# A decoder layer on one Trainium2 core: where the first two head groups are loaded, which stores a block waits for, and the order of the first instructions

## The reference

```python
# 1. mixing
pos_mem_cos = cumsum(cos(pp) * (x @ Wpv + bpv)); pos_mem_sin = cumsum(sin(pp) * (x @ Wpv + bpv))
pos_ret = (cos(pp) * pos_mem_cos + sin(pp) * pos_mem_sin) / sqrt(D)
key_ph = tanh(x @ Wk + bk) * pi
gh = gelu([x, shift(x)] @ Wg1 + bg1); gates = sigmoid(gh @ Wg2 + bg2)
kv_mem_cos = cumsum(shift(cos(key_ph)) * (x @ Wkv + bkv) * gates)      # and the same with sin
kv_ret = (cos(key_ph) * kv_mem_cos + sin(key_ph) * kv_mem_sin) / (sqrt(max(cumsum(gates), 1)) * sqrt(D))
bw = softmax(gelu(x @ Wb1 + bb1) @ Wb2 + bb2)
x + (layernorm(bw[0] * pos_ret + bw[1] * kv_ret) * ln_g + ln_b) @ Wo + bo
# 2. cross attention: 16 heads of 16, softmax over the queries
q = x @ Wq + bq; k = ctx @ Wk + bk; v = ctx @ Wv + bv
attn = softmax(q k^T / sqrt(16), axis=queries) @ v; x + attn @ Wo + bo
# 3. eight experts of width 1024, the two best of each token
sum_e w_e * (relu(x @ W1[e] + b1[e]) @ W2[e] + b2[e])
```

## Time and profile before

| what | value |
|---|---|
| median of 3 runs | 2271.31 us (2265.58 to 2274.38) |
| the profiled execution | 2271.26 us, its span 2269.6 us |
| PE busy | 1993.4 us (88%) |
| DVE busy | 1754.7 us (77%) |
| ACT busy | 1548.2 us (68%) |
| POOL busy | 727.7 us (32%) |
| granted TensorE clock, mean | 0.947 |
| moved | 212.39 MB, mean 94 GB/s |
| last chain of work | PE 24%, DVE 2% of the span; all its costlier lines are of the expert stage |

### The profile page before, as it was taken

The page is one execution under the profiler, slowest core; times in us unless marked ns, Lnnn a source line. Parts: engine busy times, 40 slices in busy tenths (PEclk is TensorE's granted clock), DMA queues, the critical chain, the costliest instruction groups (busy, mean ns, idle before and its releaser), DMA issues. The chain is left out here.

```text
span 2269.6 us, 43525 instructions
## 1 busy us (share of the span) xinstructions
PE 1993.4 (88%) x10630; PEld 1048.6 (46%) x10638; DVE 1754.7 (77%) x3559; ACT 1548.2 (68%) x4361; POOL 727.7 (32%) x967
## 2 busy tenths in 40 slices
PE   6999898499999999999999998887637999999993
PEld 2454455223222232222322221113536999999993
DVE  4989885399999999999999999996444555555554
ACT  3565565399999999999999999996212333333334
POOL 0112112044444434444344441110553333333331
PEclk9989999699999999999999999999868999999997
DMA  4111104846675665766667666652751222222224
GB/s 151 42 42 70 56 24 139 166 80 105 129 132 109 125 103 128 131 113 129 97 132 126 115 118 86 117 68 81 220 131 29 35 37 37 36 36 37 35 37 160
DMA packets 126117, 212.39 MB, mean 94 GB/s; under 512 B 31554, under 2 KB 94786, under 8 KB 124882
## 3 DMA queue, kind: packets, MB, share of 16 engines
q1 hardware_dynamic: 98272, 151.74, 36.6%
q0 software_dynamic: 26240, 59.00, 9.9%
q10 hardware_dynamic: 1554, 1.05, 0.2%
HBM read 138.38 MB, written 73.74 MB: 93 GB/s over the span
## 5 line engine op out<-in xcount | busy, mean ns | idle before, releaser
L1400 ACT ACTIVATE w_all<-psum,neg_max 128x512 f32<-128x512 f32 (+1 forms) x1664 | 1111.4, 737 | 46.3 <-DVE neg_max L1308 44.4
L1308 DVE TENSOR_REDUCE neg_max<-psum 128x1 f32<-128x512 f32 (+1 forms) x1664 | 1025.3, 676 | 18.5 <-PE psum L1245 14.9
L1245 PE MATMUL psum<-qst,kst 96*128 96x512 bf16 (+1 forms) x1664 | 530.3, 391 | 98.2 <-ACT w_all L1400 61.0
L1213 PE MATMUL psum<-w_all 128*32 128x512 f32 (+1 forms) x3328 | 450.5, 615 | 9.8 <-DVE w_all L1322 9.8
L1245 PEld LDWEIGHTS psum<-qst,kst 96*128 96x128 bf16 (+1 forms) x1664 | 130.0, 98 | 686.9 <-ACT w_all L1400 641.3
L1400 ACT ACTIVATION_READ_ACCUMULATOR w_all<-psum,neg_max 128x1 f32 (+1 forms) x1664 | 428.3, 257 | 0.0
L1734 ACT ACTIVATE hid<-psum,b 128x128 f32<-128x128 f32 x568 | 161.9, 368 | 378.3 <-PE psum L1679 374.0
L1372 POOL TENSOR_TENSOR w_all<-vst,inv 128x64 f32<-128x64 f32 (+1 forms) x416 | 121.0, 291 | 687.5 <-DVE inv L1276 686.7
L1679 PE MATMUL psum<-xst,w 128*128 128x128 f32 x2272 | 267.9, 277 | 0.0
L1679 PEld LDWEIGHTS psum<-xst,w 128*128 128x128 f32 x2272 | 262.0, 194 | 0.1
L1689 PE MATMUL psum<-area,hid 128*128 128x256 f32 x1136 | 256.9, 379 | 0.0
(11 more groups left out here) (208 smaller groups left out, 1885.2 us busy)
## 6 DMA issues: line engine op xcount, KB each, us to landing
kst<-k_parts SPq DMA_DIRECT2D x384, 112.0 KB, 6.5
k_parts<-k_out POOLq DMA_DIRECT2D x52, 336.0 KB, 3.2
w_all<-in_W SPq DMA_DIRECT2D x16, 1024.0 KB
area<-in_ctxT SPq DMA_DIRECT2D x16, 896.0 KB, 4.7
vst<-v_all SPq DMA_DIRECT2D x64, 224.0 KB, 9.2
qst<-q_parts SPq DMA_DIRECT2D x192, 64.0 KB, 5.9
v_all<-area POOLq DMA_DIRECT2D x13, 896.0 KB, 4.3
q_parts<-q_out POOLq DMA_DIRECT2D x24, 256.0 KB, 3.0
```

Source lines behind the costliest of these rows:

```text
L1213: last = pe.matmul(psum[j * PAD:(j + 1) * PAD, 6, :], v_scaled[0:r, pb, j, :], probs_at[pb][0:r, j, :], start=t == 0, stop=t == ST - 1)
L1245: pe.matmul(psum[0:r, 2 * sbuf + i, :], kst[:, h, j, t * P:t * P + r], qst[:, h, j, :], start=True, stop=True).then_inc(scores_ready, 1)
L1308: v.tensor_reduce(neg_max[0:r, sbuf, i:i + 1], psum[0:r, 2 * sbuf + i], AX_X, ALU.min) \
L1400: act.activation(probs_at[pb][0:r, j, :], psum[0:r, 2 * sbuf + i, :], ACT.Exp, bias=neg_max[0:r, sbuf, i:i + 1], scale=-1.0, accum_out=sum ...
```

## The change

- `load_heads` is split in `load_queries_keys` and `load_values`. In the mixing stage SP now loads queries and keys of group 0 of batch 0 ahead of the value stores, its values behind them; group 1 is loaded at the head of SP's list in the attention stage.
- SP no longer waits for the third unit's stores at the end of mixing, nor POOL for those of q and x1; these waits stand in the attention stage (SP ahead of its loop, POOL ahead of its own). The third unit's key pieces have buffers of their own in the region of W1 (`k_buf`), and `k1_out` is allocated last.
- The loads at the start are in two lists, `weights` (cols, the transposed x of batch 0, Wpv, Wk) and `more_weights`; x of batch 0 comes after both. PE begins with the position projection, DVE with the position angles, ACT with their sines; `wo` is scaled and centred inside DVE's first step, the means are in bank 0.
- Two semaphores of the last norm are replaced by ones of the second.

```diff
+            load_queries_keys(sp, b, g)
+            load_values(sp, b, g)
+        def load_queries_keys(sp, b, g):
...
+        def load_values(sp, b, g):
+            h = g % 2
...
+                     + [w1_all[:, i // C, i % C, 0:N_K] for i in range(KJ)]]
+            def k_buf(n):
+
+                return n % K_BUFS if n < 2 * KJ else K_BUFS + n - 2 * KJ
...
+                (xt[:, 0, :, 1:L + 1], a["xT"][0]),
+                (wpv[:], a["Wpv"].rearrange("(c p) d -> p c d", p=P)),
                 (wk[:], a["Wk"].rearrange("(c p) d -> p c d", p=P)),
+            ]
+            more_weights = [
                 (wg1[:], a["Wg1"].rearrange("(c p) d -> p c d", p=P)),
                 (wb1[:], a["Wb1"].rearrange("(c p) d -> p c d", p=P)),
-                (wpv[:], a["Wpv"].rearrange("(c p) d -> p c d", p=P)),
                 (wkv[:], a["Wkv"].rearrange("(c p) d -> p c d", p=P)),
-                (wo, a["Wo"].rearrange("(c p) d -> p c d", p=P)),
+                (wo[:], a["Wo"].rearrange("(c p) d -> p c d", p=P)),
                 (wq[:], a["xWq"].rearrange("(c p) d -> p c d", p=P)),
...
-                    load(0, 0)
+                    sp.sem_inc(xt_loaded[0], 16)
                     for tile, src in weights:
                         sp.dma_start(tile, src).then_inc(weights_loaded, 16)
+                    for tile, src in more_weights:
+                        sp.dma_start(tile, src).then_inc(more_loaded, 16)
+                    sp.dma_start(xin[:, 0].rearrange("p t d -> p (t d)"), a["x"][0]).then_inc(xt_loaded[0], 16)
                     load(1, 1)
...
-                        kb, (co, half) = n % K_BUFS, divmod(j, 2)
+                        kb, (co, half) = k_buf(n), divmod(j, 2)
                         sp.wait_ge(k_lo, n + 1)
                         sp.dma_start(k_parts[:, u, co * P:(co + 1) * P, half * KC:(half + 1) * KC]
-                                     .rearrange("n p s -> p n s"), k_out[kb]).then_inc(k_stored[kb], 16)
+                                     .rearrange("n p s -> p n s"), k_out[kb]).then_inc(k_stored[n % K_BUFS], 16)
...
                     sp.dma_start(ct[:, 0], a["ctxT"][2].rearrange("c p s -> p c s")).then_inc(ct_loaded[0], 16)
+                    for i in range(K_BUFS):
+                        sp.wait_ge(k_stored[i], 32)
+                    sp.wait_ge(q_stored, 16 * PARTS)
+                    load_queries_keys(sp, 0, 0)
                     for u in range(2):
                         store_v(u)
-
-                    for i in range(K_BUFS):
-                        sp.wait_ge(k_stored[i], 32)
                     for u in range(2):
                         sp.wait_ge(v_stored[u], 16)
-                    sp.wait_ge(q_stored, 16 * PARTS)
-                    for g in range(2):
-                        load_heads(sp, 0, g)
+                    load_values(sp, 0, 0)
                     for n in range(2 * KJ, 3 * KJ):
                         store_k(n)
                     store_v(2)
-                    for i in range(K_BUFS):
-                        sp.wait_ge(k_stored[i], 48)
-                    sp.wait_ge(v_stored[0], 32)
...
-                    pool.wait_ge(q_stored, 16 * PARTS * B)
-                    pool.wait_ge(x1_stored, 16 * B)
...
-                        if not (isinstance(b, int) and b == 0):
-                            wait(pe, q_split, PARTS * (b - 1))
+                        if isinstance(b, int) and b == 1:
+                            pe.wait_ge(wo_ready, 1)
+                        else:
+                            pe.wait_ge(q_split, PARTS * (b - 1))
...
                     pe.wait_ge(weights_loaded, 16 * len(weights))
                     pe.wait_ge(consts_made, 1)
-                    pe.wait_ge(xt_loaded[0], 32)
+                    project(5, wpv, now(0), C).then_inc(pv_ready, 1)
                     project(0, wk, now(0), C).then_inc(kz_ready, 1)
+                    pe.wait_ge(more_loaded, 16 * len(more_weights))
                     project(2, wg1, now(0), 2 * C).then_inc(gh_ready, 1)
                     blend(0, 0)
-                    project(5, wpv, now(0), C).then_inc(pv_ready, 1)
-
+                    pe.wait_ge(phase_ready, 1)
                     pe.wait_ge(derived_ready, 1)
+                    pe.wait_ge(wo_scaled, 1)
                     for k in range(C):
-                        pe.matmul(psum[:, 7, 0:D], mean_w[:], wo_c[:, k, :], start=k == 0, stop=k == C - 1)
+                        pe.matmul(psum[:, 0, 0:D], mean_w[:], wo_c[:, k, :], start=k == 0, stop=k == C - 1)
                     for k in range(C):
-                        last = pe.matmul(psum[:, 7, D:2 * D], lnb_wide[:, k, :], wo[:, k, :],
+                        last = pe.matmul(psum[:, 0, D:2 * D], lnb_wide[:, k, :], wo[:, k, :],
                                          start=k == 0, stop=k == C - 1)
                     last.then_inc(wo_mean_ready, 1)
                     gates(0, 0)
-                    pe.wait_ge(wo_ready, 1)
                     blend_weights(0, 0)
...
-                        wait(act, k_stored[kb], 16 * (n // K_BUFS))
+                        kb, u, j = k_buf(n), *K_ORDER[n]
+                        if kb < K_BUFS:
+                            wait(act, k_stored[kb], 16 * (n // K_BUFS))
...
+                    act.preload_act_table_set("trig_and_small")
+                    act.wait_ge(consts_made, 1)
+                    act.wait_ge(pos_ready, 1)
+                    act.activation(pos_sin[:], pos[:], ACT.Sin)
+                    act.activation(pos_cos[:], turns[:], ACT.Sin, bias=half_pi[:], scale=-1.0).then_inc(trig_ready, 1)
+                    act.preload_act_table_set("gelu_and_others")
                     act.wait_ge(weights_loaded, 16 * len(weights))
-                    act.wait_ge(consts_made, 1)
                     act.wait_ge(derived_ready, 1)
-                    act.preload_act_table_set("gelu_and_others")
                     phases(0)
                     gelus(0)
                     blend_gelu(0)
                     gate_of(0)
-                    act.wait_ge(pos_ready, 1)
-                    act.activation(pos_sin[:], pos[:], ACT.Sin)
-                    act.activation(pos_cos[:], turns[:], ACT.Sin, bias=half_pi[:], scale=-1.0).then_inc(trig_ready, 1)
...
                 def _(v):
+                    v.wait_ge(pos_loaded, 16)
+                    v.tensor_scalar(turns[:], pos[:], 1.0 / TWO_PI, ROUND, ALU.mult, ALU.add).then_inc(dve_pos, 1)
+                    v.wait_ge(dve_pos, 1)
...
+                    def scale_wo():
+                        v.wait_ge(more_loaded, 16 * len(more_weights))
+                        for k in range(C):
+                            last = v.tensor_scalar(wo_c[:, k, :], wo[:, k, :], col(LNG + k), None, ALU.mult)
+                        last.then_inc(wo_scaled, 1)
+                    def centre_wo():
+                        v.wait_ge(wo_mean_ready, 1)
+                        v.wait_ge(consts_loaded, N_CONSTS)
+                        for k in range(C):
+                            v.tensor_tensor(wo_c[:, k, :], wo_c[:, k, :], psum[:, 0, 0:D], ALU.subtract)
+                        v.tensor_tensor(bo_half[:], rows[:, BO, :], psum[:, 0, D:2 * D], ALU.add).then_inc(wo_ready, 1)
+                        v.wait_ge(wo_ready, 1)
+                        v.tensor_scalar(bo_half[:], bo_half[:], 0.5, None, ALU.mult).then_inc(wo_ready, 1)
...
-                        if not end or mix:
-                            pass
+                        if not end:
+                            scale_wo()
...
+                        if not end:
+                            centre_wo()
...
                     opened(sp, *attn_stored)
                     load_context(FIRST_UNITS)
+                    load_heads(sp, 0, 1)
                     sp.dma_start(list_all, a["no_pairs"]).then_inc(list_cleared, 16)
                     sp.dma_start(x2_rows[TOKENS:TOKENS + P], a["no_rows"]).then_inc(list_cleared, 16)
                     for e in range(W2_EARLY):
                         load_w2(sp, e)
+                    for i in range(K_BUFS):
+                        sp.wait_ge(k_stored[i], 48)
+                    sp.wait_ge(v_stored[0], 32)
+                    sp.wait_ge(q_stored, 16 * PARTS * B)
+                    sp.wait_ge(x1_stored, 16 * B)
...
                     pool.sem_inc(items_read, 1)
+                    pool.wait_ge(q_stored, 16 * PARTS * B)
```

64 lines of the change are left out of this document (26 added, 38 removed).

## The result

| | before | after |
|---|---|---|
| median of 4 runs | 2271.32 us (2265.58 to 2274.38) | 2238.82 us (2228.43 to 2243.18) |
| ratio, 95% interval | | 0.9853 (0.9812 to 0.9894) |
| profiled execution, span | 2271.26, 2269.6 us | 2243.18, 2241.5 us |
| PE, DVE, ACT busy | 1993.4, 1754.7, 1548.2 us | 1995.0, 1755.3, 1549.9 us |
| granted clock, mean | 0.947 | 0.948 |

A forecast was written before the change was run, and what follows sets the result against it. It took two idle stretches as the bound: PE's wait for all weights and SP's queue before attention. Gains of 25.7 and 14.1 us, plus 0.5 for the first scores, gave 2271.3 - 40.3 = 2231.0 us, range 2223 to 2243.

The forecast's parts named there:

- Beginning: Start of the kernel: PE needs only four loads before its first matmul, so DVE's kv product starts 14.1 us earlier.
- Landed at 9.8: Start: cols, xT, Wpv and Wk, 1.06 MB, taken as landed at 9.8 us, with 9.3 and 10.9 as ends.
- PE gains at least as much as DVE: Start: PE's next 28 matmuls begin at 40.8 instead of 52.69, so PE's gain at least matches DVE's 14.1 us.
- The change moves nothing: Stage from 16.7 to 407.9 us: nothing moves except in its first and last step.
- Hand-over: End of mixing to attention: SP's queue no longer holds the block's end, first score at 410.0 instead of 435.74, gain 25.7 us.
- two value stores ... landed about 401 to 402: Hand-over: value stores issued about 385.7 and 389.0, 0.92 MB each at 361 GB/s, 5.1 us, behind the 18 loads.
- cover 2 us, the thinnest: Attention's start: fourth unit's context asked for at 408.8, landed about 415, needed by PE at 417.3.
- The first group's values come late: Rival at the hand-over: value loads land at 415.5, first score slips by 5.5 us, 2236.5 us; chance 0.14.
- the fourth unit's context late too: Attention's start, added to the late-values rival: context lands at 421, 4 us more, 2241 us; within that rival's chance 0.14.
- The start gives half: Rival at the start: late loads, PE's wait for five others or late Wo scaling leave 7 us, 2238; chance 0.09.
- the gap only moves: Rival in attention: head 1 is not there at 446, costing 7 us or up to 25.7, 2257 us; chance 0.03.
- slower: Rival in attention: PE stands at tile 13 for head 1's 20 loads, 52 us beyond 446, to pass 2283; chance 0.02.

The follow-up runs named there:

- the filler: Five extra 256-column matmuls on PE before the transposes of each middle mixing step; 2206.88 us in the changed kernel, 2239.61 us in the kernel before.
- queries and keys early: Changed kernel with the first head group's 18 query and key loads moved ahead of the third unit's context load and the wait before it; 2209.89 us.
- key stores early: Changed kernel with the third unit's four key stores moved ahead of SP's wait for the value stores; 2209.11 us.
- late constants: Changed kernel with ACT's nine constant loads issued only once the first weights have landed; 2206.27 us.

## Why the prediction was right, and where it was not

The sign and the two gains held, and so did the range: 2238.82 lies in 2223 to 2243. Part of that is luck. The experts gave 4.1 us that nobody forecast; without them the profiled execution would have taken 2247, outside it. The forecast's centre was 7.7 us too fast, and the likeliest case was not what happened. Step by step:

- **Beginning, 14.1 us; got 12.7 (12.1 at the kv product).** "Landed at 9.8" was mis-sized: 11.06, just beyond the upper end given, 10.9. I counted the bytes of SP's queue ahead of Wk and left out ACT's constants, which share the DMA engines. With them out of the way it is 7.97, below my lower end. From first matmul to kv product I had 27.2 us, measured 28.1. And "PE gains at least as much as DVE" does not follow from my own numbers: 28 matmuls at 40.8 instead of 52.69 are 11.9 us, not 14.1. They began at 40.62, and the first mixing product follows them on PE with no stop for DVE, so PE's gain was the one to count. The five other weights and DVE's parts were hidden, as said.
- **"The change moves nothing" in the stage between: failed, +4.8 us.** The instructions did not move, their times against the clock did: three long steps instead of one, shown by the filler in both kernels.
- **Hand-over, 25.7 us; got 22.5.** The failing step is "two value stores ... landed about 401 to 402", 6 us ahead of the last copy. Against the last copy the loads began 3.6 us later than I had put them (27.6 us ahead instead of 31.2), and store landings took 1.8 us more than my sum: 1 us ahead was left. Of the 3.6 us, 3.3 are the clock: I took the distance from a trace in which the stretch ahead of the context ran at 1.00, and now it ran at 0.79. My 1.4 us from issue to first bytes came from no row; before, the DMA engines stood at 0.00 from 376.3 to 377.3, 1.0 us. Behind it I had let SP's seven issues go for nothing; through a full queue they took until 403.33.
- **The fourth unit's context, "cover 2 us, the thinnest": gone.** I costed 6.2 us from issue to landing and it took 12.6: it stands behind the stores, which begin later than I had them, with head group 1's 18 loads issued right behind it. Price 4.0 us in the row and 5.2 to the first stored head, instead of a gain of 0.5.
- **The rivals.** "The first group's values come late" with "the fourth unit's context late too", at chance 0.14, said 2241 and has the size of what came: slips of 3.3 and 4.0 us where it had 5.5 and 4. Its second half happened as told, the context's 12.5 us included, and I had that row and preferred rates. Its first half did not: the value loads took 2.7 us, not 13.5, and the first score waited for the block's end. What was late was SP, held by the value stores. "The start gives half", "the gap only moves" and "slower" did not come: head group 1 never made PE wait.
- **Ends of the range.** 2231 - 3 and + 5 are 2228 and 2236, where I wrote 2225 and 2237, and the first two rivals together, the late context included, come to 2247 by their own prices, not 2243. The range was a little too wide below and too narrow above.
- **Rules.** The projections behind 40.62 run at 0.44 us each, so the 1.9 us did go with the 5.06 us stop, as I had allowed from the row. It gave 0.6 us by the first mixing product and nothing by the end. The Trainium skill (TensorE: Matmul & The Clock Gate, Part 1) has idleness drop the clock, and for that stop the trace agrees, 0.53 us a matmul behind it, at a mean granted clock of 0.83, and 0.44 without it, at 1.00; the stops of 1.4 and 4.8 us in the middle steps remained, and I did not ask where the slow spell would fall once the step's rhythm changed. The Trainium skill (DMA: Bandwidth & Descriptors, Queues, rings and completion order) has a transfer's semaphore write land, on each DMA engine, only after that engine's earlier writes; the value stores, issued behind the 18 loads, landed so, 13.0 and 16.3 us after their issue.

In numbers: -12.7 + 4.8 - 22.5 + 5.2 + 1.2 - 4.1 = -28.1 between profiles, against -40.3.

Open: why the new beginning makes steps long more often (sums of 292.7 to 296.1 us in its nine traces without filler, 290.4 and 291.2 in the two with the old one). The filler shows where the slow spell may fall without harm; what fixes its place in a given step was not tried. The context's lateness is split only in part. With head group 1's loads right behind it as before, it lands in 7.7 us (queries and keys early), 7.9 (filler) and 9.5 (key stores early), so those loads alone don't make it late. But with late constants it takes 12.2 and PE stops for 4.02 us, though the gap is 2.40 there too; what decides between them stays open.

## What to carry to other kernels

- When a list of transfers is moved to where it is needed, check what else fills the engines there. Here it paid to ask for 18 slow loads 13 us before the stretch in which they compete, not to reorder within it; each reordering there made the value loads late instead.
- When a transfer waits for a stretch of PE's work, its distance from what follows is no constant: 13.3 us at a granted clock of 1.00 was 16.6 at 0.79. Look at the clock of that stretch before you take a cover from it.
- Count all queues when timing a first load, those of engines that do not wait for it too. In a cover of 2 us reckoned from mean rates, put the slowest landing that the trace shows for that size and queue state, and let it decide which case is likeliest.
- Where an engine stops for some us in each turn of a loop, look at its granted clock in the work right behind the stop, turn by turn. If turns have two lengths, the place of the slow spell is a suspect, and a little harmless work in the stop tests it.

## What the runs showed that was not expected

- More PE work, less time: with 2.32 us of extra matmuls in each of six steps the seven steps took 9.8 us less (296.0 to 286.2). Some 0.9 us of it came ahead of the first filler.
- The identical kernel took 2238.82 us when first measured and 2215.24 on chip B, with the same ratio to the kernel before (0.9853, 0.9851). Of 23.5 us between the two traces 20.1 are in the expert stage, and its first part holds them. Windows of its first 200 us, first measurement:

```profile
1544.00:1744.00 200.00, 123.80 (x710) 111.59 (x711) 88.20 (x400) 47.29 (x121) 83.95 (x82) 0.76 0.50 132
```

and chip B:

```profile
1541.00:1741.00 200.00, 144.01 (x852) 129.97 (x853) 99.47 (x420) 54.19 (x145) 90.69 (x88) 0.82 0.53 136
```

PE gets through 852 matmuls instead of 710. What makes the difference was not tried; where it was looked up, the first measurement and chip A show 120 to 127 us of PE busy in these windows, chip B 143 to 147. A time without a run of the kernel before on the same chip says nothing within 1%.
- Issuing is no constant: the third value store took 1.30 us to issue into the full queue at 402.03, and 0.38 in the kernel whose queries and keys went early.
